# Finishing by whole chunks: one subtraction and one scaling per chunk, statistics from accumulator outputs

## The reference

```python
xn = batch-style pre-normalisation of x, then layernorm over channels
left  = (xn @ Wl + bl) * sigmoid(xn @ Wlg + blg)      # times a mask in layers 0 and 2
right = (xn @ Wr + br) * sigmoid(xn @ Wrg + brg)
out   = einsum over the shared index k of left and right, per channel
out   = layernorm(out) (scale ow, shift ob)
x     = x + (out * gate) @ Wo + bo                    # layers 0 and 1: gate before Wo
x     = x + (out @ Wo + bo) * gate                    # layers 2 and 3: gate after Wo
```

## Time and profile before

| | |
|---|---|
| median of 3 runs | 2437.58 us (2436.82 to 2440.13) |
| profiled execution | 2443.13 us, its span 2441.1 us |
| mean granted TensorE clock | 0.942 of 2.4 GHz |
| busy, share of the span: PE, DVE, ACT, POOL | 82%, 86%, 65%, 44% |
| finish of layer 0 | from 488.6 us to 673.3 us of the span |
| finish of layer 1 | 1077.6 to 1262.3 us |
| finish of layer 2 | 1693.5 to 1874.6 us |
| finish of layer 3 | 2278.2 us to the end |

### The profile page before, as it was taken

How to read it: one execution, slowest core, us unless ns; L and a number is a source line. 1 busy time by engine, 2 the same in 40 slices (tenths; PEclk the granted TensorE clock), 3 DMA queues, 4 the chain that set the end, 5 groups by cost and what they waited for, 6 DMA issues and landing times. The chain is left out here.

```text
span 2441.1 us, 50395 instructions
## 1 busy us (share of the span) xinstructions
PE 2011.7 (82%) x13892; PEld 1388.7 (57%) x13892; DVE 2091.0 (86%) x3053; ACT 1579.3 (65%) x2341; POOL 1081.9 (44%) x804
## 2 busy tenths in 40 slices
PE   4598969477789898977779889897777988989798
PEld 3433959233333698953333388885333338888465
DVE  5699999899979987879979997876998999787676
ACT  2487789554468777754448776764444888686576
POOL 0077839077657200026747782540443770000476
PEclk8799989699999899989999999998999999999899
DMA  8776837789768848489946682839996788394997
GB/s 331 288 244 238 284 116 245 216 253 330 251 188 255 280 137 275 144 336 369 370 171 240 241 281 82 282 112 337 330 345 236 231 246 298 111 304 163 360 420 297
DMA packets 370777, 624.57 MB, mean 256 GB/s; under 512 B 17520, under 2 KB 246896, under 8 KB 354288
## 3 DMA queue, kind: packets, MB, share of 16 engines
q1 hardware_dynamic: 368368, 606.55, 72.4%
q10 hardware_dynamic: 2304, 16.78, 1.6%
HBM read 413.54 MB, written 209.72 MB: 255 GB/s over the span
## 5 line engine op out<-in xcount | busy, mean ns | idle before, releaser
L696 PE MATMUL bank<-whigh,obuf 128*128 128x128 f16 x4096 | 511.3, 228 | 77.4 <-DMA obuf<-XH 41.4
L696 PEld LDWEIGHTS bank<-whigh,obuf 128*128 128x128 f16 x4096 | 469.2, 126 | 84.0 <-issue 58.6
L613 POOL TENSOR_TENSOR LR<-LR 128x1024 f32<-128x1024 f32 x128 | 374.8, 2929 | 313.9 <-ACT LR L604 313.9
L696 PE MATMUL bank<-wlow,obuf 128*128 128x128 f16 x4096 | 510.6, 228 | 0.0
L696 PEld LDWEIGHTS bank<-wlow,obuf 128*128 128x128 f16 x4096 | 469.6, 126 | 0.0
L832 PE MATMUL bank<-LR 128*128 128x256 f32 (+1 forms) x1792 | 378.9, 375 | 30.6 <-DVE LR L761 16.0
L1146 POOL TENSOR_TENSOR LR<-LR,sum 128x512 f32<-128x512 f32 x128 | 208.6, 1638 | 416.0 <-DVE LR L1177 411.5
L832 PEld LDWEIGHTS bank<-LR 128*128 128x128 f32 (+1 forms) x1792 | 321.8, 181 | 85.6 <-ACT obuf L844 20.9
L1068 PE MATMUL bank<-kst,LR 128*128 128x128 f32 x1024 | 167.0, 287 | 160.6 <-POOL LR L1146 96.3
L575 PE MATMUL bank<-LR,cen 128*128 128x512 f32 x512 | 260.9, 635 | 44.3 <-DVE LR L623 41.1
L1068 PEld LDWEIGHTS bank<-kst,LR 128*128 128x128 f32 x1024 | 116.5, 144 | 309.4 <-POOL LR L1146 174.8
(11 more groups left out here) (115 smaller groups left out, 3615.0 us busy)
## 6 DMA issues: line engine op xcount, KB each, us to landing
LR<-XT SPq DMA_DIRECT2D x128, 512.0 KB, 5.3
obuf<-XH SPq DMA_DIRECT2D x128, 512.0 KB, 5.0
LR<-XT SPq DMA_DIRECT2D x64, 1024.0 KB, 9.3
obuf<-XHA SPq DMA_DIRECT2D x128, 512.0 KB, 4.6
XT<-obuf SPq DMA_DIRECT2D x48, 1024.0 KB, 9.5
OS<-obuf SPq DMA_DIRECT2D x24, 2048.0 KB, 8.1
LR<-OS SPq DMA_DIRECT2D x96, 512.0 KB, 8.1
LR<-XH SPq DMA_DIRECT2D x128, 256.0 KB, 6.4
```

The lines of the kernel that those rows point to most:

```text
L613: pool.tensor_tensor(yc[k], yc[k], rs[k], ALU.mult).then_inc(normed.s, 1)
L696: last = pe.matmul(bank(g)[:, j * P:(j + 1) * P], tokens, w[:, half * P:(half + 1) * P], start=part == 0, stop=part == 1)
```

## The change

- nrm keeps the column order (s c v) of OS. One `center` (layers 0 and 1) or one `normalize` (layers 2 and 3) on VectorE treats a whole chunk of 2048 columns; in layers 0 and 1 one GpSimd instruction multiplies a whole chunk. GpSimd subtracts nothing any more. Layers 0 and 1 have four nrm buffers.
- `turn` picks the tile's columns out of nrm with a stride of 16 fp32 elements (the view n_t); the transposed rows come out in the order (s c), and the parameters, the gate's weights and wout_c are laid out for it.
- Layers 0 and 1 turn into four PSUM banks; `scale_shift` works in place there, and `gate` reads its first input from PSUM.
- `count` is dropped in layers 0 and 1. `add` writes the sum of the new x by an accumulator output, and ScalarE gets a third operation, `square`, whose accumulator output is the sum of (x - m)^2, with m the mean that entered the layer (shift). `prepare` of layers 1 and 2 makes mean and variance of these sums.
- Lags: in layers 0 and 1 `gate` 7, `add` 9, `square` 7 on ScalarE; in layers 2 and 3 `gate_late` 6, `count` 8.
- SP's `next_inputs` waits for the chunk's `center` (layers 0 and 1) or `normalize`.

```diff
+            from_sums = number > 0 and LAYERS[number - 1]["gate_first"]
+            total, squared_total = small[:, 8:9], small[:, 9:10]
...
+                    if from_sums:
+                        dve.reduce_sum(total, stats[:, :, 0:1].rearrange("p t o -> p (t o)"),
+                                       mybir.AxisListType.X).then_inc(summed_up.s, 1)
+                        dve.reduce_sum(squared_total, stats[:, :, 1:2].rearrange("p t o -> p (t o)"),
+                                       mybir.AxisListType.X).then_inc(summed_up.s, 1)
...
+                    else:
+                        dve.bn_aggr(small[:, 0:2], stats[:, :, :].rearrange("p t f -> p (t f)")).then_inc(step.s, 1)
...
+                    dve.tensor_scalar(shift, mean, -1.0, None, ALU.mult)
...
-            nrm = [flat[:, c * COLS:(c + 1) * COLS] for c in (10, 11)]
-            gated = [flat[:, 14 * COLS + c * BANK:14 * COLS + (c + 1) * BANK] for c in range(4)]
+            nrm = [slot(c) for c in ((10, 11, 14, 15) if gate_first else (10, 11))]
...
-            aff, og = ([v[:, c * BANK:(c + 1) * BANK] for v in ring for c in range(2)] for ring in rings)
+            ring0, og = ([v[:, c * BANK:(c + 1) * BANK] for v in ring for c in range(2)] for ring in rings)
+            aff, gated = (None, ring0) if gate_first else (ring0, [slot(14)[:, c * BANK:(c + 1) * BANK] for c in range(4)])
             o_v = [o.rearrange("p (s c v) -> p s c v", s=2, c=C) for o in o_f]
-            n_v = [o.rearrange("p (v c s) -> p s c v", s=2, c=C) for o in nrm]
+            n_v = [o.rearrange("p (s c v) -> p s c v", s=2, c=C) for o in nrm]
+            n_t = [o.rearrange("p (w v) -> p w v", v=16) for o in nrm]
+            turn_bank = (lambda k: bank((0, 1, 6, 7)[k % 4])) if gate_first else (lambda k: bank(k % 2))
+            consumed = mean_off if gate_first else normalized
...
-            fed, taken, aff_used = (gated_ready, x_ready, gated_ready) if gate_first else (scaled, gated_ready, out_projected)
-            PO, GL, AL, CL, TB, TBA = (3, 3, 5, 6, 0, 0) if gate_first else (2, 4, 0, 6, 5, 4)
+            fed, taken = (gated_ready, x_ready) if gate_first else (scaled, gated_ready)
+            SL = 7
+            PO, GL, AL, CL, TB, TBA = (3, 7, 9, 0, 0, 0) if gate_first else (2, 6, 0, 8, 5, 4)
...
-                        sp.wait_ge(normalized.s, normalized.n + 16 * i + 4 * h + 4)
+                        sp.wait_ge(consumed.s, consumed.n + 4 * i + h + 1)
...
-                        pe.wait_ge(normalized.s, normalized.n + tile + 1)
-                        pe.wait_ge(scaled.s, scaled.n + tile - 1)
+                        if q == 0:
+                            pe.wait_ge(normalized.s, normalized.n + 4 * i + h + 1)
+                        if gate_first:
+                            pe.wait_ge(gated_ready.s, gated_ready.n + tile - 3)
+                        else:
+                            pe.wait_ge(scaled.s, scaled.n + tile - 1)
                         for j in range(4):
-                            last = pe.transpose(by_token(bank(k % 2))[:, :, j, :],
-                                                nrm[h % 2][:, (4 * q + j) * P:(4 * q + j + 1) * P], K(K_IDENT))
+                            last = pe.transpose(by_token(turn_bank(k))[:, :, j, :],
+                                                n_t[h % len(nrm)][:, :, 4 * q + j], K(K_IDENT))
...
-                        act.wait_ge(aff_used.s, aff_used.n + tile - 3)
                         if gate_first:
-                            act.activation(aff[k % 4], bank(k % 2), ACT.Identity, bias=vec(V_OB),
+                            act.activation(turn_bank(k), turn_bank(k), ACT.Identity, bias=vec(V_OB),
                                            scale=vec(V_OW)).then_inc(scaled.s, 1)
                         else:
-                            act.activation(aff[k % 4], bank(k % 2), ACT.Copy).then_inc(scaled.s, 1)
+                            act.wait_ge(out_projected.s, out_projected.n + tile - 3)
+                            act.activation(aff[k % 4], turn_bank(k), ACT.Copy).then_inc(scaled.s, 1)
...
+                    def square(i, k):
+                        h, q = divmod(k, 4)
+                        act.wait_ge(x_ready.s, x_ready.n + 16 * i + k + 1)
+                        act.wait_ge(stats_taken.s, stats_taken.n + 16 * i + k)
+                        act.activation(sum1[:, :, N:2 * N].rearrange("p t (g f) -> p t g f", f=64),
+                                       pair_cols(xo[h % depth], q).rearrange("p (t g) f -> p t g f", t=2),
+                                       ACT.Square, bias=shift,
+                                       accum_out=stats[:, bass.ds(16 * i + k, 1), 1:2].rearrange("p o f -> p (o f)")) \
+                            .then_inc(stats_taken.s, 1)
+
-                    pipeline(act, rounds, 16, (scale_shift, 0), (sigmoid, 0), *([(back, TBA)] if end else []))
+                    pipeline(act, rounds, 16, (scale_shift, 0), (sigmoid, 0), *([(square, SL)] if gate_first else []),
+                             *([(back, TBA)] if end else []))
...
...
+                    def normalize(i, h):
+                        pool.wait_ge(mean_off.s, mean_off.n + 4 * i + h + 1)
+                        pool.tensor_tensor(n_v[h], n_v[h], token(sum2, i, h), ALU.mult).then_inc(normalized.s, 1)
...
                     def center(i, k):
-                        if k % 4 == 3:
+                        if k % 4:
                             return
+                        h = k // 4
+                        dve.wait_ge(landed[h].s, landed[h].n + 32 * i + 32)
+                        dve.wait_ge(turned.s, turned.n + 16 * i + k - 12)
+                        dve.wait_ge(normalized.s, normalized.n + 4 * i + h)
+                        dve.tensor_tensor(n_v[h], o_v[h], token(sum1, i, h), ALU.subtract).then_inc(mean_off.s, 1)
 
                     def normalize(i, k):
+                        if k % 4:
+                            return
+                        h = k // 4
+                        dve.wait_ge(landed[h].s, landed[h].n + 32 * i + 32)
+                        dve.wait_ge(turned.s, turned.n + 16 * i + k - 4)
+                        dve.tensor_tensor(n_v[h % 2], o_v[h], token(sum2, i, h), ALU.mult).then_inc(normalized.s, 1)
 
                     def gate(i, k):
...
-                        dve.tensor_tensor(gated[k % 4], aff[k % 4], og[k % 4], ALU.mult).then_inc(gated_ready.s, 1)
+                        dve.tensor_tensor(gated[k % 4], turn_bank(k), og[k % 4], ALU.mult).then_inc(gated_ready.s, 1)
...
+                            dve.wait_ge(stats_taken.s, stats_taken.n + 16 * i + k - 12)
                         dve.wait_ge(out_projected.s, out_projected.n + 16 * i + k + 1)
                         dve.scalar_tensor_tensor(pair_cols(xo[h % depth], q), tall(bank(4 + k % 2)), vec(V_BO),
-                                                 pair_cols(xi[h], q), ALU.add, ALU.add).then_inc(x_ready.s, 1)
+                                                 pair_cols(xi[h], q), ALU.add, ALU.add,
+                                                 accum_out=stats[:, bass.ds(16 * i + k, 1), 0:1]
+                                                 .rearrange("p o f -> p (o f)")).then_inc(x_ready.s, 1)
...
-                        pipeline(dve, rounds, 16, (center, 0), (gate, GL), (add, AL), (count, CL))
+                        pipeline(dve, rounds, 16, (center, 0), (gate, GL), (add, AL))
```

More of the change, by code:

```diff
@@ L60 @@
 X_SCALE = 1024.0
+TOKENS = N * N // 2
 W_SCALE = 1024.0
@@ L327, in on_pe @@
                 if late:
-                    pe.matmul(bank(6)[:, 0:P], K(K_CENTER), wout_w, start=True, stop=True)
+                    pe.matmul(bank(6)[:, 0:P], K(K_CENTER_OUT), wout_w, start=True, stop=True)
                     pe.matmul(bank(7)[:, 0:1], w_out, vec(V_OB), start=True, stop=True).then_inc(late_folded.s, 1)
@@ L513, in _ @@
                 def _(dve):
-                    dve.bn_aggr(small[:, 0:2], stats[:, :, :].rearrange("p t f -> p (t f)")).then_inc(step.s, 1)
+                    if from_sums:
[3 more added lines that the diff above has]
+                                       mybir.AxisListType.X).then_inc(summed_up.s, 1)
+                        dve.wait_ge(summed_up.s, summed_up.n + 1)
+                        dve.tensor_scalar(mean, total, 1.0 / TOKENS, None, ALU.mult).then_inc(step.s, 1)
+                        dve.tensor_scalar(dev, total, 1.0 / TOKENS, shift, ALU.mult, ALU.add).then_inc(summed_up.s, 1)
+                        dve.wait_ge(summed_up.s, summed_up.n + 3)
+                        dve.scalar_tensor_tensor(second, dev, -1.0, dev, ALU.mult, ALU.mult).then_inc(summed_up.s, 1)
+                        dve.wait_ge(summed_up.s, summed_up.n + 4)
+                        dve.scalar_tensor_tensor(var, squared_total, 1.0 / TOKENS, second, ALU.mult, ALU.add) \
+                            .then_inc(summed_up.s, 1)
+                        dve.wait_ge(summed_up.s, summed_up.n + 5)
```

(12 more changed lines are left out.)

49 lines of the change are left out of this document (14 added, 35 removed).

## The result

The kernel after takes 2378.46 us (median of 4 runs, 2376.36 to 2381.84), that before 2438.86 beside it on the same chip (2436.82 to 2443.3). The ratio is 0.9751, 95% interval 0.9733 to 0.977: 60 us faster, where 51 were forecast, and inside the forecast's range of 2355 to 2450. The profiled execution has 2376.36 us and a span of 2374.5.

The account below looks back on a forecast made before the run. VectorE was taken to bound the finishes of layers 0 to 2, TensorE layer 3, transfers close behind. Layers 0 to 3 gave -24, -29, -21, +23, prepare 0: -51 us, 2392, or 2387 on the median's scale; 8-in-10 range 2355 to 2450.

Parts of the forecast that it names:

- Limits: Finishes of layers 0 to 2: transfers, at 10 to 12.1 us a chunk, hide compute of 8 to 9.2 us.
- Costs on VectorE: VectorE per chunk after the change: 8.1 us, at most 9.9, in layers 0 and 1; 7.4 us in layer 2.
- Strided loads: Transposes loading one fp32 column per 64 bytes cost TensorE 0.35 us a tile; layer 3 gets 22 us longer from it.
- The pitch of the earlier trace: Layers 0 and 1's f16 project loads: pitch 56 to 63 ns; for strided transposes a lower bound of 0.03 us a tile.
- the prediction's own sign: Transpose pitch on TensorE near 0.2 us expected; the prediction is wrong if it stays at 0.11 or passes 0.26.
- The first rival, hidden loads: Strided loads cost 0.03 us a tile; layers 0 to 2 give 74 us, layer 3 loses 3: 2366 us; chance 0.32.
- the sum: Layer 2's finish: last XT issue at 1838.59 stays, + 9.3 + 4 x 1.27 + 0.7 = 1853.7, against 1874.58: -21 us.
- Instead of running down four buffers: Stages of layers 0 to 2 end once the last XT load has landed and four tiles are added.
- another of the prediction's signs: Layers 0 and 1, where GpSimd multiplies by chunk: the prediction is wrong if VectorE waits for GpSimd.
- Lags and SP's prefetch depth: Layers 0 and 1 fill about 4 us later, 2 us for the first finished chunk; one lost prefetch chunk costs nothing.
- The loop as bound: Layers 0 and 1: subtraction, multiply, subtraction keeps about 11 us a chunk if GpSimd exceeds 8 us: 2440; chance 0.06.

Follow-up runs that it names:

- the halved XH: Finishes load only the first of XH's two f16 parts and use it for both: 2314.0 us in the kernel after, 2425.9 us in the kernel before.
- the old lags: Kernel after with gate 3 and add 5 tiles behind the subtraction (layers 0 and 1), gate 4 and count 6 (layers 2 and 3): 2521.5 us.
- SP's order, with the lags 5 and 7: Kernel after with next OS, XH, XT at distances 0, 1, 2 chunks, store before next XT, gate 5 and add 7 behind (layers 0, 1): 2340.4 us.
- the lags 4 and 6: Kernel after with gate 4 and add 6 tiles behind the subtraction in layers 0 and 1, instead of 7 and 9: 2419.9 us.

## Why the prediction was right, and where not

- *Limits.* Right that the transfers take over in layers 0 to 2; the halved XH shows it (-49 us in these finishes after, nothing before). The rates were read well: 421 and 347 GB/s in layers 1 and 2, where 376 to 418 and 346 were taken.
- *Costs on VectorE.* Subtraction taken as 2.4 us, measured 2.21 start to start; add 0.65 + 0.15, measured 0.67; gate 0.62, measured 0.60. So 7.3 us a chunk where 8.1 was taken. Multiply 5.1 to 6.5 taken, 4.55 measured: below the lower end. ScalarE: 1.95 us a tile (three instructions, 1129.75 to 1131.70), 7.8 a chunk, the lower of the two values.
- *Strided loads: the step that failed.* "I take 0.35" us a tile; measured 0.01 (2.38 to 2.39). The load did lengthen by 50 ns, as the earlier trace rows had it, but the prediction added what a load's duration has over a transpose's 0.11 us, as if a load had to end before its transpose may start. The records of layer 3 overlap instead: the loads start 0.11 us apart and last 0.193. The pitch of the earlier trace rows, 7 ns, was the part to believe. The 64 x 0.35 = 22 us of layer 3 did not come. By the prediction's own sign (wrong if the pitch stays at 0.11) this step is refuted. The first rival, hidden loads, was the true mechanism, though its 2366 is farther from 2378 than the forecast: other terms made up for it.
- *Luck.* Against the forecast layer 3 lost 22 us less and layer 2 gained 9 less; the rest differs by 3 or 4 each. That the total came within 9 us is owed in part to errors of opposite sign.
- *Layer 2: the term that was mis-sized.* The last XT goes 146.4 us after the stage's start, where 145.1 was forecast; so pace and limit were right. But its tail, 15.1 us in the sum, is 23.0. The adds of chunk 14 wait for the store that frees their buffer, the late one of chunk 10, and those of chunk 15 follow without a wait for the last load.

```profile
1778.75 2.50 POOL L1186 TENSOR_TENSOR obuf<-LR 128x512 f32<-128x512 f32 x2 [4.27 <-DMA XT<-obuf]
1784.45 2.52 POOL L1186 TENSOR_TENSOR obuf<-LR 128x512 f32<-128x512 f32 x2 [3.19 <-DVE LR L1238]
1791.05 9.92 POOL L1186 TENSOR_TENSOR obuf<-LR 128x512 f32<-128x512 f32 x8 [4.08 <-DMA XT<-obuf]
```

  Eight adds follow 1791.05, where the sum had four (+4.8 us), and 3.3 us pass between the last count and prepare, which the sum didn't have.
- *Layers 0 and 1: two errors that cancel.* The pace is 9.7 and 9.1 us, where 10.7 and 10.0 to 10.9 were taken, but the tails behind the last XT issue are 25.1 and 31.9 us, not 15.3. "Instead of running down four buffers" was wrong: after XT of chunk 15 has been asked for, 13 tiles are still to be added in layer 0 and 16 in layer 1, at some 1.95 us each. XT is asked for when chunk 11 is finished (0.1 us later in layer 1), or later where SP is behind (7.0 us in layer 0). The waits fall on OS (16.8 us in layer 0), not on XT. By another of the prediction's signs VectorE was not to wait for GpSimd; it does for 8.1 us in three waits of layer 0, the longest 4.7, which is small beside the pace.
- *Lags and SP's prefetch depth, costed at nothing.* Near enough for the total, but three things were missed: the lead is what makes chunks possible at all (+70 us a layer at the old lags); SP falls behind by its own issues, up to 32 us in layer 2, and not by waiting for x; and SP's order, with the lags 5 and 7, was worth 38 us more.
- *The loop as bound* (rival at 2440): not here, since 2.3 + 4.55 = 6.9 us is under the transfers; with the lags 4 and 6 a longer loop, through TensorE's projection and the add, comes in fact, at 2420.

## What to carry to other kernels

Before an operation is made coarser, look up which instruction in the other engines' program order stands behind its result: the lag has to cover that order, here four tiles plus the projection's three, and one tile short of it costs 20 us a layer. When a stage passes from an engine to the transfers, engine terms stop adding up, and it is the order of loads and stores in the issuing queue that is worth trying next. For the tail of a prefetched stage, count the tiles that must still be computed once the last transfer has been asked for, and look whether the issuing queue waits for work or is late by itself.

## What the runs showed of the hardware

- A 128x128 fp32 weight load with its columns 64 bytes apart takes 193 ns instead of 140 in the records, and costs 3 ns of pitch in a row of transposes of 0.11 us each: loads start 0.11 us apart and their records overlap.
- The accumulator's read takes 0.08 us on VectorE and 0.20 on ScalarE by the records; start to start the add takes 0.67 us with it, 0.65 without.
- GpSimd's multiply: 4.55 us for 2048 columns, 1.14 for 512 of them. In instructions of 512 columns it took 1.64 on average and 1.29 at least, beside VectorE's.
- With the path of the transfers full, SP's issue of 256 KB of XH takes up to 5.4 us in layer 2, and 0.61 to 0.64 for the first eight of that stage.
- With the store ahead of the load of XT the same transfers ran at 373 instead of 336 GB/s in layer 0, and no row says why.
